# State-space stage: the row normalisation in another place of VectorE's order, its mean square from ScalarE

## What is computed

```python
def _layernorm(x, axis=-1, eps=1e-05):
    m = jnp.mean(x, axis=axis, keepdims=True)
    v = jnp.var(x, axis=axis, keepdims=True)
    return (x - m) / jnp.sqrt(v + eps)
...
def _rmsnorm(x, w):
    return x * jax.lax.rsqrt(jnp.mean(x * x, axis=-1, keepdims=True) + EPS) * w
...
residual = x
xn = _rmsnorm(x, norm_weight)
y_fwd = _mamba2(xn, fwd_W_in, ...)
y_bwd = jnp.flip(_mamba2(jnp.flip(xn, 1), bwd_W_in, ...), 1)
out = jnp.concatenate([y_fwd, y_bwd], axis=-1) @ proj_W.T + proj_b
return residual + out
...
x = x + _L1_attn_ref(_layernorm(x, axis=-1), ...)
```

## Time and profile before

| | |
|---|---|
| median of 3 runs | 4094.79 us (4093.77 to 4096.73) |
| the profiled execution | 4099.99 us, span 4098.0 us |
| busy over the span | TensorE 94%, VectorE 73%, ScalarE 69%, GpSimd 46% |
| state-space stage, about | 2533 to 3320 us of the span |
| one step in the loop of that stage | 12.0 us and 12.5 us in turn |

### The profile page before, as it was taken

One profiled execution on the slowest core, in us unless ns is written; L12 is line 12 of the kernel. 1 busy time (PEld: TensorE's weight loads), 2 busy tenths in 40 slices (PEclk: granted clock), 3 DMA queues, 4 the chain that ended last, 5 costly groups with the idle time before them and its releaser, 6 DMA issues. The chain is left out here.

```text
span 4098.0 us, 106550 instructions
## 1 busy us (share of the span) xinstructions
PE 3856.6 (94%) x33992; PEld 2995.1 (73%) x33992; DVE 3004.8 (73%) x7523; ACT 2829.1 (69%) x6420; POOL 1878.4 (46%) x1792
## 2 busy tenths in 40 slices
PE   7999899999979999898999989999999989998999
PEld 5666688888746666685666677888888867776777
DVE  7888655555569999658999955777777767776665
ACT  5666455555569999757999965777777757775333
POOL 5444322222268888526777753333333321112443
PEclk9999899999999999999999999999999989999999
DMA  0000100000000000100000010000000000000000
GB/s 19 9 9 10 48 8 6 6 6 6 26 25 8 8 8 8 27 17 10 8 8 8 14 27 29 1 0 0 0 0 0 0 3 4 3 3 6 12 12 12
DMA packets 109258, 42.46 MB, mean 10 GB/s; under 512 B 91232, under 2 KB 107872, under 8 KB 108512
## 3 DMA queue, kind: packets, MB, share of 16 engines
q1 hardware_dynamic: 109152, 41.10, 3.9%
HBM read 20.16 MB, written 4.19 MB: 6 GB/s over the span
## 5 line engine op out<-in xcount | busy, mean ns | idle before, releaser
L1152 POOL TENSOR_TENSOR l_rc<-l_rc,l_rs 128x1024 f32<-128x1024 f32 x128 | 303.7, 2373 | 201.5 <-DVE l_rs L1344 201.5
L1219 ACT ACTIVATE l_prob<-l_prob,l_mx 128x128 f32<-128x128 f32 x1024 | 312.0, 389 | 0.0
L1830 POOL TENSOR_TENSOR mb_steps<-w_upto,mb_dta 128x1024 f32<-128x1024 f32 x64 | 121.5, 1898 | 353.7 <-DVE mb_dta L2087 353.7
L721 POOL TENSOR_TENSOR ca_prob<-ca_prob,ca_sm 128x1232 f32<-128x1232 f32 x64 | 144.0, 2250 | 299.3 <-DVE ca_sm L887 299.3
L1244 PE MATMUL l_qk_ps<-w_local,l_hT 128*128 128x512 f32 x512 | 248.9, 609 | 13.4 <-DVE l_rs L1344 11.4
L1146 POOL TENSOR_TENSOR l_prob<-l_prob,l_sm 128x1024 f32<-128x1024 f32 x128 | 243.0, 1899 | 18.4 <-DVE l_sm L1330 18.4
L1129 POOL TENSOR_TENSOR l_rc<-l_rc,l_ss 128x1024 f32<-128x1024 f32 x128 | 243.6, 1903 | 12.5 <-POOL l_rc L1152 4.5
L1987 PE MATMUL mb_x_ps<-w_wx,mb_xT 128*128 128x256 f32 x1024 | 237.2, 385 | 0.0
L2552 POOL TENSOR_TENSOR mo_hid<-mo_hid,mo_gate 128x1024 f32<-128x1024 f32 x64 | 121.8, 1903 | 199.4 <-DVE mo_hid L2698 199.4
L1339 DVE TENSOR_REDUCE l_ss<-l_sq 128x16 f32<-128x1024 f32 x128 | 156.1, 1219 | 77.8 <-ACT l_sq L1183 77.4
L1987 PEld LDWEIGHTS mb_x_ps<-w_wx,mb_xT 128*128 128x128 f32 x1024 | 190.2, 191 | 23.3
(11 more groups left out here) (355 smaller groups left out, 12065.8 us busy)
## 6 DMA issues: line engine op xcount, KB each, us to landing
la_xin<-in_x SPq DMA_DIRECT2D x64, 64.0 KB
l_h<-lt_y SPq DMA_DIRECT2D x128, 32.0 KB
lt_quad<-lt_y SPq DMA_DIRECT2D x32, 128.0 KB
out_x<-k_x SPq DMA_DIRECT2D x64, 64.0 KB, 1.5
l_h<-lt_y SPq DMA_DIRECT2D x128, 31.8 KB
lt_quad<-lt_y SPq DMA_DIRECT2D x32, 127.0 KB
ca_ctxT<-in_ctx_T SPq DMA_DIRECT2D x128, 19.2 KB
wr_state<-in_p_state SPq DMA_DIRECT2D x1, 2438.5 KB, 11.9
```

The costliest lines, as they stand in the source:

```text
L721: gp.tensor_tensor(prob[b.slot][:], prob[b.slot][:], sm[b.lane][:, 1].unsqueeze(2).to_broadcast([T, H, S]), ALU.mult).then_inc(*pool_prob. ...
L1152: gp.tensor_tensor(wide(rc[l][:]), wide(rc[l][:]), wide(rs[l][:]), ALU.add).then_inc(*pool_sum.did("rot"))
L1219: ex = sc.activation(p[:, a, j], p[:, a, j], ACT.Exp, bias=mx[l][:, a, j:j + 1])
```

## The change

The mean square of a row, var / (var + eps), was one VectorE instruction (L2116) from the reciprocal root of ScalarE; it went back to ScalarE for Ln and Exp. Now ScalarE makes a second exponential of the same logarithm with the scale -1 (`rvar`, 1 / (var + eps)) right behind the first, and the Ln behind it takes the variance with that number as its scale, so VectorE's instruction is gone. The first norm r moves from behind xb up to the start of softplus, right behind L2124, ahead of the wait for ScalarE's exponential. The second norm xn moves from behind xb into `softplus`, between the eighth step of the convolution and dta.

```diff
-        vec_norm = Stage(m.sem("vec_norm"), "stats mv q r xn")
+        vec_norm = Stage(m.sem("vec_norm"), "stats mv r xn")
...
-        act_norm = Stage(m.sem("act_norm"), "lnv rstd lnq rms")
+        act_norm = Stage(m.sem("act_norm"), "lnv rstd rvar lnq rms")
...
                         sc.activation(rstd[l][:, 1:2], rstd[l][:, 0:1], ACT.Exp, scale=-0.5).then_inc(*act_norm.did("rstd"))
+                        sc.activation(rstd[l][:, 2:3], rstd[l][:, 0:1], ACT.Exp, scale=-1.0).then_inc(*act_norm.did("rvar"))
...
-                        sc.wait_ge(*vec_norm.at("q", b))
-                        sc.activation(rms[l][:, 1:2], rms[l][:, 0:1], ACT.Ln, bias=eps[:]).then_inc(*act_norm.did("lnq"))
+                        sc.wait_ge(*act_norm.at("rvar", b))
+                        sc.activation(rms[l][:, 1:2], mv[l][:, 1:2], ACT.Ln, scale=rstd[l][:, 2:3], bias=eps[:]
+                                      ).then_inc(*act_norm.did("lnq"))
...
+                def normalised(b):
+                    l = b.lane
+                    v.wait_ge(*vec_norm.at("r", b))
+                    v.wait_ge(*act_norm.at("rms", b))
+                    v.wait_ge(*pe_turn.at("xT", b, ago=2))
+                    v.tensor_scalar(xn[l][:], r[l][:], rms[l][:, 2:3], None, ALU.mult).then_inc(*vec_norm.did("xn"))
+
-                def softplus(b, seg):
+                def softplus(b, seg, norm):
...
                     beside()
+                    if norm:
+                        normalised(norm)
                     v.wait_ge(*vec_dt.at("dt", b))
...
-                    b = at(NORM)
-                    if b:
-                        l = b.lane
-                        v.wait_ge(*act_norm.at("rstd", b))
-                        v.scalar_tensor_tensor(out=rms[l][:, 0:1], in0=rstd[l][:, 1:2], scalar=rstd[l][:, 1:2],
-                                               in1=mv[l][:, 1:2], op0=ALU.mult, op1=ALU.mult).then_inc(*vec_norm.did("q"))
```

More of the change, by code:

```diff
@@ L1740, in mamba @@
         r, xn = both(m, "r", [T, C]), both(m, "xn", [T, C])
-        stats, mv, rstd = both(m, "stats", [T, 6]), both(m, "mv", [T, 2]), both(m, "rstd", [T, 2])
+        stats, mv, rstd = both(m, "stats", [T, 6]), both(m, "mv", [T, 2]), both(m, "rstd", [T, 3])
         rms = both(m, "rms", [T, 3])
@@ L2125, in step @@
                                                op0=ALU.mult, op1=ALU.min).then_inc(*vec_dt.did("av"))
+                    b = at(NORM)
+                    if b:
+                        l = b.lane
+                        v.wait_ge(*act_norm.at("rstd", b))
+                        v.wait_ge(*pool_norm.at("xr", b, ago=2))
+                        v.tensor_scalar(r[l][:], one(b), mv[l][:, 0:1], rstd[l][:, 1:2], ALU.subtract, ALU.mult
+                                        ).then_inc(*vec_norm.did("r"))
                     b = at(PROJ)
                     if b:
-                        softplus(b, at(SEG))
-                    elif at(SEG):
-                        decayed(at(SEG))
+                        softplus(b, at(SEG), at(NORM))
+                    else:
+                        if at(SEG):
+                            decayed(at(SEG))
+                        if at(NORM):
+                            normalised(at(NORM))
                     b = at(PROJ)
@@ L2136, in step @@
                         v.tensor_tensor(two(xs[l][:]), x_ps[:], two(cbx), ALU.add).then_inc(*vec_x.did("xb"))
[L2137 to L2141, removed]
-                                        ).then_inc(*vec_norm.did("r"))
-                        v.wait_ge(*vec_norm.at("r", b))
-                        v.wait_ge(*act_norm.at("rms", b))
-                        v.wait_ge(*pe_turn.at("xT", b, ago=2))
-                        v.tensor_scalar(xn[l][:], r[l][:], rms[l][:, 2:3], None, ALU.mult).then_inc(*vec_norm.did("xn"))
                     b = at(OUT)
```

## The result

| | before | after |
|---|---|---|
| median of 4 runs | 4095.76 us (4093.77 to 4097.54) | 4070.31 us (4068.64 to 4072.93) |
| the profiled execution | 4099.99 us, span 4098.0 us | 4072.93 us, span 4071.2 us |
| one step of the state-space loop | 12.0 and 12.5 us in turn | 11.83 us, every step |

The ratio is 0.9937, 95% interval 0.9925 to 0.9949: faster by 25.5 us, where 23.3 had been worked out. The time foretold was 4071.5 us. One execution of all that follow, of the kernel with the long clearing, came at a granted clock of 0.65 with 5437.81 us and is in none of the figures.

The account below looks back on a forecast made before the run. TensorE, busy 697.37 of 710 us in the state-space loop, was taken as the bound, so VectorE counts only where TensorE waits. -9.4 - 13.9 = -23.3 us from the median 4094.8 gave 4071.5 us, range 4067 to 4087.5.

Parts of the forecast that it names:

- The wait: TensorE's transpose in the state-space loop no longer waits for VectorE's k_x: -9.4 us.
- The branch: At trip ends TensorE reads the loop's branch early, under matmuls, saving 0.48 us at each of 29: -13.9 us.
- Part 1: VectorE's r, moved up into a gap before ScalarE's exponential, takes 0.34 us and costs the chain 0 to 0.1 us.
- The slower rival: r meets GpSimd's xdt, delaying softplus, SiLUs and xT until TensorE waits: 20 us slower, 4115 us; chance 0.06.
- Part 2: Removing VectorE's mean square, ahead of an operation that waits for TensorE's dt product anyway: 0 to -0.1 us.
- Part 3: xn ahead of dta adds at most 0.29 us; xb 0 to 0.1 us later, steps covered by 0.9 us.
- The 0.6 us feared at the stage's start: In the stage's first steps GpSimd's steps can come last; two such steps would cost 0.6 us, left to the range.
- Part 4: VectorE's k_x ends 1.33 us after xb's start, 1.2 to 1.3 us before the transpose: wait gone, -9.4 us.
- Part 6: ScalarE's idle 0.81 us covers the added exponential, 0.20 us or less; xT up to 0.35 us later, 1.0 us cover left.
- the one in which k_x is not what is last: Rival: something else holds the transpose to its old time; with no gain left 4094.8 us, chance 0.07.
- The one in which the branch stays: Rival: the 0.48 us restart at trip ends comes whether TensorE waited or not; only the wait goes, 4085.4 us, chance 0.17.

Follow-up runs that it names:

- the long clearing: The changed kernel with an idle VectorE clearing of 128x1280 unused elements ahead of the output's additions in every step: 4085.43 us, ratio 0.9973.
- half of steps: The kernel before, VectorE's order unchanged, with GpSimd's steps operation cut to one of two directions (128x512 for 128x1024): 4071.39 us, ratio 0.9936.
- the first experiment: The kernel before with only the mean square moved to ScalarE, both norms left behind xb: 4095.69 us beside 4095.34, ratio 1.000.
- r alone: The kernel before with only r moved up to softplus; xn stays behind xb, the mean square on VectorE: 4078.24 us, ratio 0.9958.
- the wait taken away: The kernel before, VectorE's order unchanged, with the transpose writing free columns of g's bank, so without its wait for k_x: 4068.52 us, ratio 0.9935.

## Why the prediction held, point by point

- **The wait** (-9.4 us, with the 0.17 us taken off that stand there without a wait): the transpose has 0.17 us before it in all 58 steps and waits for nobody. The size is right. The 9.4 counted the 56 steps of the loop's stretch, and a few steps outside it gain as well.
- **The branch** (-13.9 us, taken in full between 0 and -13.9): gone in full. The reason, that k_x's lead of 1.2 us is more than twice the 0.55, was the right comparison, and the runs give the bound for it: 0.6 us. The reading that TensorE stands still and only then reads on is what the sequencer's own instructions show. Of the 0.61 us the compare-and-branch itself is 0.215, about twice the figure that the prediction cites; it rightly went by the row.
- **Together** -23.3 us; the stage became 24.6 us shorter. In the loop the fit is closer: two steps went from 11.99 + 12.50 = 24.49 us to 23.66, 0.83 less, where 2 x 0.17 + 0.48 = 0.82 had been counted. Over 29 trips that is 24.1 us; the sum had 23.3 because it counted 56 waits and not 58, and rounded. The remaining 0.5 us lie in the steps outside the loop.
- **Part 1, r:** 0.34 us, in the gap ahead of ScalarE's exponential. It was put at 0 to 0.1 us on the chain; the next operation starts 0.06 behind the exponential where it started 0.03 behind it before. xdt ends at 2913.63 + 1.04 = 2914.67, 0.11 us ahead of r, and between 0.10 and 0.14 ahead in the loop but for two steps at the start, where r began 0.05 before its end and took 0.34 all the same. The slower rival was further off than that: with half of steps r started 0.24 us before GpSimd had ended and still took 0.34.
- **Part 2, the mean square:** 0, as the first experiment shows. Its 0.21 to 0.65 us lay ahead of an operation that waits for TensorE's dt anyway. It was held too: in 59 steps of before it ended 0.01 to 0.02 us behind xdt. The second operation of softplus was held in two steps of the kernel after (0.75 and 0.35 us for 0.17) and in one of the kernel before (0.76), so this hold was hardly handed on.
- **Part 3, xn:** 0.28 us, ahead of dta. VectorE's idle time before xb (0.19 in the earlier trace rows) is gone, but xb is hardly later: in both kernels it starts 0.04 us behind the last matmul of x in nearly every step. It was counted at 0 to 0.1. steps ends at 2920.01 + 1.90 = 2921.91, 0.94 us ahead of the load that needs it at 2922.85; 0.9 had been given. The 0.6 us feared at the stage's start can't be seen in the stage's total.
- **Part 4, k_x:** 1.34 us behind xb's start for 1.33; its lead is 1.34 for 1.2 to 1.3.
- **Part 6, ScalarE:** xT ends at 2911.97 and TensorE reads it at 2913.27, a cover of 1.30 us for the 1.0 foretold; the shift of ScalarE was smaller than its bound. ScalarE's idle time before L1875 went from 0.81 to 0.58, the price of the exponential and r together. How much more ScalarE could take was not tried.
- **The rivals:** the one in which k_x is not what is last is out, with k_x 1.34 us ahead and no wait in its place; the slower one is answered under part 1. The one in which the branch stays would have shown steps of 11.8 and 12.3 in turn, and needs a lead under 0.6 us: the kernels with r alone and with the long clearing are that case (steps of 11.83 and 12.13, 11.83 and mostly 12.26). That the mean square or less work on VectorE brought something is excluded by the first experiment.
- **What the prediction didn't see:** that xn, left behind xb, would be held by GpSimd in r's place. It prices xn at 0.29 us; left behind xb without r, xn took 0.99 to 1.29 us in 62 of 64 steps. r's move alone brought k_x 0.24 us (at a trip's end) ahead of the transpose and 17 of the 25 us, xn's the rest up to 1.34. The sum came out right since both moved together.

## What to carry to other kernels

Ask of a wait on TensorE not only how long it is but what stands behind it: with the loop's branch next, 0.16 us of waiting cost 0.64 (0.16 + 0.48). A wait that is over 0.6 us before its instruction is due costs neither; one that is just over in time saves the wait and leaves the branch. And read an operation's duration beside GpSimd's: r, xn and the mean square, short VectorE operations with nothing in PSUM, lasted until the GpSimd one that they started within had ended, so taking one such operation away can only hand the delay to the next.

## What the runs showed of the hardware

- **The branch behind a wait.** From the end of a wait of a weight load, over the loop's branch, to the next weight load it takes 0.61 us (0.61 or 0.62 by the rounded rows), in four kernels with leads of 0.06 to 0.57 us; without a branch between them 0.13. TensorE's sequencer goes on 0.05 us behind the semaphore's last operation, even where the load itself starts later (2914.49 and 2914.68 with r alone). Its compare-and-branch takes 0.215 us; those of GpSimd and ScalarE take 0.045 at the same line (kernel before). Work that TensorE has queued ahead of the waiting load covers all of it.
- **GpSimd's hold.** A VectorE operation of 0.34 or 0.29 us (one SBUF tensor, scalars per row) took 1.01, 1.18 or 1.29 us when it started within GpSimd's steps, by how early it started, and each time ended 0.08 or 0.09 us behind it: 2912.04 and 2911.96 in the earlier trace rows, 2913.79 and 2913.71 with r alone, 2906.29 and 2906.20 with the wait taken away. The same operation took 0.34 when steps was half as long. The Trainium skill (SBUF — State Buffer, SBUF: two separate sides) states such a lock, with the later of the two fully blocked; the four cases agree. acc and k_x, which read PSUM, kept their 0.34 and 0.35 us within steps (2920.77 and 2921.15 in the kernel after).
- **A wait below what the list shows.** dt's wait for gm left 0.04 us of idle time and was in no list of waits, but it cost 0.11 us a step, since the load did not overlap the one ahead of it (by 0.07 us at its later place, by 0.11 in the one step that has no gm).
